# The first of two expert routers: fetching token rows per expert instead of scattering them to slots

## The reference

```python
h = layernorm(x) * (1 + cb) + sb
logits = h @ gate_weight.T                      # 8 experts
probs = softmax(logits)
top1 = argmax(logits)
mask = one_hot(top1, E)
ranks = cumsum(mask, axis=0) - 1                # place of a token in its expert's list
mask = mask * (ranks < C)                       # C = 320 slots per expert, the rest is dropped
dispatch[e, rank] = h[token]                    # 8 x 320 rows
eout = gelu(dispatch @ wi[e]) @ wo[e]           # 256 -> 1024 -> 256
x = x + gb * (probs[top1] * eout[e, rank])      # kept tokens only
```

## Time and profile before

| what | value |
|---|---|
| timed runs, us | 1158.65, 1157.9, 1160.58; median 1158.65 |
| profiled execution, us | 1162.2 |
| its span, first to last instruction, us | 1160.4 |
| TensorE busy | 980.0 us (84%) |
| VectorE busy | 632.0 us (54%) |
| ScalarE busy | 534.2 us (46%) |
| GpSimd busy | 297.8 us (26%) |
| mean granted TensorE clock | 0.929 |

### The profile page before, as it was taken

How to read it: one execution, slowest core, us unless ns; L and a number is a source line. 1 busy time by engine, 2 the same in 40 slices (tenths; PEclk the granted TensorE clock), 3 DMA queues, 4 the chain that set the end, 5 groups by cost and what they waited for, 6 DMA issues and landing times. The chain is left out here.

```text
span 1160.4 us, 24988 instructions
## 1 busy us (share of the span) xinstructions
PE 980.0 (84%) x9918; PEld 635.9 (55%) x9923; DVE 632.0 (54%) x1714; ACT 534.2 (46%) x830; POOL 297.8 (26%) x344
## 2 busy tenths in 40 slices
PE   5889899999999999957099999558657599999994
PEld 3433334445444444433067777346435599999993
DVE  4257999999799797746000000284766533333331
ACT  3523567777866866644023231075055343333330
POOL 3001330011001121320511213245720144545442
PEclk9987999999999999998599999769788799999998
DMA  5753000000002003019315454300055623222223
GB/s 159 174 129 54 2 3 2 3 3 3 2 3 94 3 3 3 3 31 363 99 23 168 108 177 107 84 1 1 0 185 197 209 42 50 45 50 45 50 45 90
DMA packets 71485, 81.65 MB, mean 70 GB/s; under 512 B 21201, under 2 KB 62545, under 8 KB 70689
## 3 DMA queue, kind: packets, MB, share of 16 engines
q1 hardware_dynamic: 58576, 62.75, 19.1%
q0 software_dynamic: 12288, 17.10, 8.4%
q10 hardware_dynamic: 528, 0.52, 0.1%
HBM read 58.19 MB, written 24.13 MB: 71 GB/s over the span
## 5 line engine op out<-in xcount | busy, mean ns | idle before, releaser
L579 ACT ACTIVATE k_prob<-f_s 128x1024 f32<-128x1024 f32 (+3 forms) x320 | 270.1, 896 | 118.5 <-PE f_s L427 117.9
L639 DVE TENSOR_REDUCE k_mpart<-f_r 128x1 f32<-128x512 f32 x384 | 250.6, 685 | 31.7 <-PE f_r L370 29.4
L370 PE MATMUL f_r<-k_ks,k_qs 112*32 112x512 bf16 (+3 forms) x2560 | 212.0, 359 | 16.2 <-DVE k_mpart L639 7.3
L427 PE MATMUL f_s<-k_qs,k_ks 114*32 114x512 bf16 (+3 forms) x2560 | 173.9, 350 | 1.9 <-ACT k_prob L579 1.3
L841 POOL TENSOR_SCALAR_AFFINE_SELECT k_prob<-k_prob 128x256 f32<-128x256 f32 x128 | 51.2, 406 | 400.1 <-ACT k_prob L579 398.9
L443 PE MATMUL f_o<-k_prob,k_vaug 128*32 128x512 f32 (+3 forms) x1280 | 146.5, 531 | 1.5 <-POOL k_prob L841 1.4
L370 PEld LDWEIGHTS f_r<-k_ks,k_qs 112*32 112x32 bf16 x2560 | 69.1, 96 | 135.1 <-DVE k_mpart L639 56.2
L636 DVE CUSTOM_DVE_ANT_0 k_unread<-f_r,k_causal 128x128 bf16<-128x128 f32 (+3 forms) x256 | 121.2, 484 | 21.9 <-PE f_r L370 20.9
L427 PEld LDWEIGHTS f_s<-k_qs,k_ks 114*32 114x32 bf16 x2560 | 64.2, 97 | 79.3 <-issue 27.8
L2002 DVE TENSOR_TENSOR mid<-silu_g,e_u 128x512 f32<-128x512 f32 x39 | 26.8, 688 | 124.7 <-PE e_u L1907 124.7
L1442 DVE SCALAR_TENSOR_TENSOR outr<-p_o,rows,k_mod 128x256 f32<-128x256 f32 x16 | 7.8, 484 | 140.8 <-PE p_o L1399 140.8
(11 more groups left out here) (312 smaller groups left out, 1274.6 us busy)
## 6 DMA issues: line engine op xcount, KB each, us to landing
r_raw<-in_L_ffn_w_dram SPq DMA_DIRECT2D x24, 512.0 KB, 5.8
k_wi<-in_L_ffn_wi_dram SPq DMA_DIRECT2D x8, 1024.0 KB, 5.1
k_wo_e<-in_L_ffn_wo_dram SPq DMA_DIRECT2D x8, 1024.0 KB, 7.5
k_qs<-q_dram SPq DMA_DIRECT2D x6, 768.0 KB, 9.6
sum<-k_x SPq DMA_DIRECT2D x8, 512.0 KB, 9.5
q_dram<-k_room SPq DMA_DIRECT2D x12, 256.0 KB, 4.6
disp<-k_room SPq DMA_DIRECT2D x2, 1310.0 KB, 7.0
rows<-disp SPq DMA_DIRECT2D x8, 262.0 KB, 2.6
```

What stands on the lines that cost most here:

```text
L370: last = nc.tensor.matmul(dst[32 * j:32 * (j + 1), :], qs[0:KROWS, c, GH * g + hs, q0:q0 + 32], ks[0:KROWS, QC * ck:QC * ck + w], start=Tr ...
L427: last = nc.tensor.matmul(sc[h % 2][32 * j:32 * (j + 1), i, off:QC], ks[0:KALL, k0:k0 + 32], qs[0:KALL, c, GH * g + 2 * pair + i, off:QC], ...
L579: nc.scalar.activation(prob[:, u % 2, 2 * pair:2 * pair + 2, off:QC], sc[h % 2][:, :, off:QC], ACT.Exp, scale=HD ** -0.5).then_inc(e_done, 1)
L639: nc.vector.reduce_max(mpart[:, s % 2, hs, t, ck:ck + 1], bank(r)[:, 0:w], AX.X).then_inc(ring_used[r % RING], 1)
```

## The change

The front no longer fills and stores the table `disp`. The function `phase_router` is split. The second layer keeps its part as `phase_router1`, unchanged. The first layer gets `phase_router0`:

- the normalised rows go to `k.h` and from there to `h_rows` in HBM in token order, by four SyncE stores; SyncE's order is now gate weights, expert 0's weights, `wmod`, the four stores, x to the sum, expert 1's weights, the mixing's loads;
- the greatest logit is found by reductions and comparisons over all tiles at once;
- expert and rank give every token a position in a tile of 128 slots (`pos`) and a tile (`blk`, 3 tiles for each of 8 experts); `at_pos` and `at_blk` are the one-hot forms in bf16;
- TensorE sums `at_pos` × codes over all tokens, once for the token number (two codes), once for the weight (three bf16 parts); the last 64 slots of an expert are written to partitions 64 to 127 as well, for the half-width rows of the second product;
- VectorE reads token numbers `tok0`, row numbers `row0` and weights `w0` of all slots;
- GpSimd fetches the rows of experts 0 and 1 from `h_rows` by three indirect loads each, at the end of the router.

In `phase_experts0` SyncE loads weights only, GpSimd issues the three indirect loads of expert e + 2 before the three additions of expert e, and ScalarE begins with a one-column Gelu whose result nobody reads.

```diff
-                for i in range(NT):
-                    nc.gpsimd.indirect_dma_start(
-                        out=k.disp, out_offset=bass.IndirectOffsetOnAxis(ap=scat[:, 0, i:i + 1], axis=0),
-                        in_=hx[:, i, :], in_offset=None).then_inc(sent, 16)
-                pool.wait_ge(sent, 16 * NT)
...
+def gather_rows0(nc, k, e):
+
+    s = e % 2
+    for r, (r0, rn) in enumerate(SLOT_TILES):
+        b = len(SLOT_TILES) * e + r
+        nc.gpsimd.indirect_dma_start(
+            out=k.rows0[0:rn, s, r, :], out_offset=None, in_=k.h_rows,
+            in_offset=bass.IndirectOffsetOnAxis(ap=k.tok0[0:rn, b:b + 1], axis=0)).then_inc(k.rows0_in[s], 16)
...
+            load_weights0(sp, k, a, 0, 0)
+            sp.dma_start(wmod[:, :, :], a.L1_wmod.rearrange("(t p) n -> p t n", p=P)).then_inc(wmod_in, 16)
+            hv = k.h_rows.rearrange("(i p) d -> p i d", p=P)
+            for q in range(NC):
+                sp.wait_ge(h_ready, q + 1)
+                sp.dma_start(hv[:, TQ * q:TQ * (q + 1), :], quarter(k.h, q)).then_inc(kept_h, 16)
...
+            def invert(c0, c1):
+
+                lo = inv_lo[c0][:, 0:NS0 * (c1 - c0)]
+                hi = inv_hi[c0][:, :, :].rearrange("p i e -> p (i e)")[64:128, 0:E * (c1 - c0)].rearrange("p (c e) -> p c e", c=c1 - c0)
+                for i in range(NT):
+                    rhs = code[:, i, c0:c1, :]
+                    nc.tensor.matmul(lo, at_pos[:, i, :], rhs.rearrange("p c b -> p (c b)"),
+                                     start=(i == 0), stop=(i == NT - 1))
+                    last = nc.tensor.matmul(hi, at_pos[:, i, 0:64],
+                                            rhs.rearrange("p c (e r) -> p c e r", r=NST)[:, :, :, NST - 1],
+                                            start=(i == 0), stop=(i == NT - 1), tile_position=(0, 64))
+                return last
...
+            step(nc.vector.tensor_copy(logits[:, :, :], plog[:, :, :]))
+            step(nc.vector.reduce_max(best[:, :], logits[:, :, :], AX.X))
+            step(tt(pri[:, :, :], logits[:, :, :], last_bcast(best[:, :], E), ALU.is_equal))
+            tt(diff[:, :, :], logits[:, :, :], last_bcast(best[:, :], E), ALU.subtract).then_inc(diff_ready, 1)
+            step(tt(pri[:, :, :], pri[:, :, :], bcast(desc[:, :], NT), ALU.mult))
+            step(nc.vector.reduce_max(best[:, :], pri[:, :, :], AX.X))
+            step(tt(one_hot[:, :, :], bcast(desc[:, :], NT), last_bcast(best[:, :], E), ALU.is_equal))
+            nc.vector.tensor_copy(chosen[:, :, :], one_hot[:, :, :]).then_inc(chosen_ready, 1)
...
+            step(tt(at_blk[:, :, :], bcast(iota_b[:, :], NT), last_bcast(blk[:, :], NS0), ALU.is_equal))
+            step(ts(code[:, :, 0, :], at_blk[:, :, :], tok1[:, 0:1], None, ALU.mult))
+            step(tt(code[:, :, 1, :], at_blk[:, :, :], last_bcast(iota_hi[:, :], NS0), ALU.mult))
+            tt(at_pos[:, :, :], bcast(iota_pos[:, :], NT), last_bcast(pos[:, :], P), ALU.is_equal).then_inc(pos_ready, 1)
...
+            for n in range(3):
+                last = tt(code[:, :, 2 + n, :], at_blk[:, :, :], last_bcast(w_part[:, n, :], NS0), ALU.mult)
+            last.then_inc(code_ready, 1)
...
+            dve.wait_ge(tok_done, 1)
+            read(0, 2)
+            step(stt(slot[:, :, :], inv[:, 1, :, :], float(P), inv[:, 0, :, :], ALU.mult, ALU.add))
+            step(ts(row[:, :, :], slot[:, :, :], -1.0, 0.0, ALU.add, ALU.max))
+            nc.vector.tensor_copy(k.tok0[:, :], row[:, :, :].rearrange("p e r -> p (e r)")).then_inc(tok_ready, 1)
...
+            pool.wait_ge(kept_h, 16 * NC)
+            pool.wait_ge(tok_ready, 1)
+            for e in range(2):
+                gather_rows0(nc, k, e)
...
+            nc.scalar.activation(unread[:, :], k.rstd[:, 0:1], ACT.Gelu).then_inc(gelu_done, 1)
...
+            for e in range(E):
+                s = e % 2
+                if e + 2 < E:
+                    pool.wait_ge(t_done, e + 1)
+                    gather_rows0(nc, k, e + 2)
```

More of the change, by code:

```diff
@@ L752, in _ @@
                 rows(s)
[L753 to L765, removed]
         @block.gpsimd
@@ L961, in phase_router @@
         block = ctx.enter_context(nc.Block())
-        KSEL = layer + 1
         @block.sync
@@ L1035, in _ @@
                     pe.wait_ge(hT_ready, 2 * (q - 1))
-                if layer == 1 and q == 2:
-                    pe.wait_ge(w_copied, 6)
-                for last in transpose_quarter(nc, k, rows.h, q, tp[q % 2]):
+                for last in transpose_quarter(nc, k, k.h, q, tp[q % 2]):
                     last.then_inc(tp_done, 1)
@@ L1084, in _ @@
+            pe.wait_ge(lT_ready, NC)
+            pe.wait_ge(pos_ready, 1)
+            invert(0, 2).then_inc(tok_done, 1)
+            pe.wait_ge(code_ready, 1)
+            invert(2, 5).then_inc(weight_done, 1)
         @block.scalar
         def _(act):
[L1086 to L1091 removed]
@@ L1157, in _ @@
-            if layer == 0:
-                chosen_t = one_hot[0]
-            else:
-                chosen_t = chosen
-                step(tt(chosen[:, :, :], one_hot[0][:, :, :], one_hot[1][:, :, :], ALU.add))
-            nc.vector.tensor_copy(chosen_bf[:, :, :], chosen_t[:, :, :]).then_inc(chosen_ready, 1)
-            for j in range(KSEL):
-                step(tt(tmp[j][:, :, :], logits[:, :, :], last_bcast(top[:, :, j], E), ALU.subtract))
-                nc.vector.tensor_scalar_min(tmp[j][:, :, :], tmp[j][:, :, :], 0.0).then_inc(delta_ready, 1)
@@ new lines, in _ @@
+            read(0, 2)
+            step(stt(slot[:, :, :], inv[:, 1, :, :], float(P), inv[:, 0, :, :], ALU.mult, ALU.add))
+            step(ts(row[:, :, :], slot[:, :, :], -1.0, 0.0, ALU.add, ALU.max))
+            nc.vector.tensor_copy(k.tok0[:, :], row[:, :, :].rearrange("p e r -> p (e r)")).then_inc(tok_ready, 1)
+            step(ts(taken[:, :, :], slot[:, :, :], 0.5, None, ALU.is_gt))
+            step(ts(row[:, :, NST - 1], row[:, :, NST - 1], 2.0, upper[:, 0:1], ALU.mult, ALU.add))
+            step(tt(row[:, :, :], row[:, :, :], iota_empty[:, :, :], ALU.subtract))
@@ new lines, in _ @@
+            step(tt(row[:, :, :], row[:, :, :], taken[:, :, :], ALU.mult))
+            step(tt(row[:, :, :], row[:, :, :], iota_empty[:, :, :], ALU.add))
+            step(nc.vector.tensor_copy(k.row0[:, :], row[:, :, :].rearrange("p e r -> p (e r)")))
+            dve.wait_ge(weight_done, 1)
+            read(2, 5)
+            step(tt(inv[:, 2, :, :], inv[:, 2, :, :], inv[:, 3, :, :], ALU.add))
+            step(tt(k.w0[:, :], inv[:, 2, :, :].rearrange("p e r -> p (e r)"),
+                    inv[:, 4, :, :].rearrange("p e r -> p (e r)"), ALU.add))
```

836 lines of the change are left out of this document (455 added, 381 removed).

## The result

The changed kernel took 1153.11 us (median of five runs, 1151.52 to 1153.84) against 1160.58 for the kernel before in runs on the same chip (1157.9 to 1163.96): a ratio of 0.9934, interval 0.9915 to 0.9952. That is faster by 7.5 us, where 13.4 were forecast, and 1153.11 lies outside the range 1143.0 to 1150.5. Part of the distance is the base: the forecast started from 1158.65, the median of three runs, and the kernel before measured 1.9 us more in the five runs here. A range moved up by as much would end at 1152.4, so the measured time would lie outside that too. In a second comparison the same two kernels gave 1153.36 against 1163.43, a ratio of 0.9921 (0.9897 to 0.9945); the two medians alone give 0.9913. The profiled execution took 1153.11 with a span of 1151.2 and a mean clock of 0.932.

The account below looks back on a forecast made before the run. The first router's 34.2 us wait, mostly GpSimd's scatter, was taken as the bound. Chain, inversion, gathers and barrier put the first transpose at 565.3 instead of 578.67, 13.4 us sooner: 1158.65 becomes 1145.3, range 1143.0 to 1150.5.

Parts of the forecast that it names:

- What bounds the kernel: Before the first expert's first transposes, weight loads wait 34.2 us, 20.6 of them GpSimd building scatter descriptors; not TensorE's stretch.
- Up to the position codes: First router: rank product ends at 544.65 as before, then VectorE's work puts the last position code at 552.1.
- The cover: Twelve modulation products ahead of the rank product hide that `chosen` is ready some 2 us sooner; without them 2 us gained.
- The inversion: First router: 32 short TensorE products take at most 2.7 us, hidden behind VectorE's work; token numbers at 556.0.
- The gathers: End of first router: six take 7.3 us, starting 0.5 after VectorE's last number; with 1.0 disturbance GpSimd ends at 564.8.
- the disturbance: VectorE's work beside the first router's gathers lengthens them by 1.0 us, bounds 0 and 1.4.
- The rival of GpSimd held by VectorE: First router's gathers wait until VectorE is done, from 561.5 on; gain only 9.4 us, 1149.3; chance 0.12.
- The barrier: From the gathers' end to the first transpose: 0.5 us, upper bound 1.4; first transpose at 565.3.
- Each later stage starts at a barrier after this one and is not edited: Behind the first router: whatever moves the first transpose at 578.67 moves the rest of the kernel by as much.
- The front: Kernel's start: removing a 2.28 us fill, two stores of zeros and the marks gains zero, at most 2.3 us.
- Gathers spoil the loop: Expert loop: gathers on each expert's path cost 3.8 us seven times, less the 13.4, giving 1171.8; chance 0.03.
- nothing gained: First router: modulation weights land at 552.5 instead of before 539, so the time stays 1158.65; chance 0.02.

Follow-up runs that it names:

- all_late: all_three with VectorE making the weight-code products after the token numbers and its five modulation-row operations in the expert stage: 1140.65 us.
- all_three: Changed kernel with inversion products in two runs, rank products before modulation products, one expert's rows gathered in the router, no GpSimd drain behind the front: 1140.03 us.
- late_mix: all_three with SyncE's eight loads for the mix stage issued at the start of the expert stage instead of the router: 1139.85 us.

## Why the prediction was wrong

**What bounds the kernel: right.** Before the change 34 us at this place were not TensorE's, and removing the scatter gave 9.4 us at the first transpose by two profiles of each kernel (61.99 less 52.54).

**Up to the position codes: right within 0.2 us.** The rank products and the codes came where the sum had them. The cover that the step names, the modulation products, was worth 2.6 us and not 2.

**The inversion: the largest miss, 2.3 us.** The step took 1.34 us for 32 wider products of the second router, doubled it for the lower clock, and called 2.7 an upper bound. Those 32 are all of one shape. The bound holds for one shape (1.21) or for two runs (1.75), and fails for a turn of shapes (4.95). The price of an operation was carried over without its order. Token numbers came at 558.3 in the clock of before, not 556.0.

**The gathers: 7.5 us instead of 8.3 with the disturbance.** Six of them span 7.50 us, and the first started 0.9 behind the numbers, not 0.5. Only the first is longer (1.25, in all profiles but all_late), though VectorE did only operations of 0.2 us beside it. So of the 0.67 us that the step read from the first scatter (1.63) as VectorE's doing, some 0.3 belong to any first transfer of the router; beside the modulation rows (561.87 to 564.81) they took 0.96, 0.95 and 0.91, as later in the expert stage with VectorE idle (0.96, 0.94, 0.91). Half-sized gathers are hardly cheaper, 0.91 against 0.96. The rival of GpSimd held by VectorE is refuted for the modulation rows: no gather was held for the length of a VectorE instruction. In all_late two gathers beside them took 0.08 and 0.19 us more, less than any such instruction (0.43 to 0.75). The rule of the Trainium skill, page "SBUF — State Buffer", section "Who interferes with whom", that one engine blocks fully for the other's whole instruction, was cited beside that rival. The page says so of VectorE's two-port modes alone, so 2.7 us for all five operations was more than it gives; and these rows agree with no full block for any of them.

**The barrier: 2.2 us missed.** The step took 0.42 from the second router, where GpSimd's last indirect transfer was a whole stage back, and its upper bound of 1.4 left the drain out. The experiments put the barrier at 0.54 to 0.72 and the drain behind six gathers at 1.95. Of the second router nothing could be carried over: its drain had been over for 50 us when the block ended.

**"Each later stage starts at a barrier after this one and is not edited": wrong.** The barrier's own price was changed, by eighteen more indirect transfers: a drain of 3.48 us instead of 2.02, so 1.5 us given back at the end of the expert stage. In the loop GpSimd's three more gathers per expert cost nothing, as said; their drain did.

**The front: priced at nothing, worth 2.3 us.** The prediction had it only as an upper bound, since TensorE waits for none of it.

The sum by measured terms: 13.4 − 2.3 (inversion) − 0.4 (start) + 0.8 (gathers) − 2.2 (barrier) = 9.3 at the first transpose; less 1.5 and plus 2.3 makes 10.1. The two comparisons gave 7.5 and 10.1 us by their medians, and by their intervals 5.6 to 9.9 and 6.4 to 12. The terms fit the second and lie just above the upper end of the first; what made the first lower stays open. That the forecast of 13.4 came within a factor of two of either is partly luck: 2.3 us that it had put at nothing made up for one of the terms that it missed.

**Rivals.** "Gathers spoil the loop" and "nothing gained" did not happen. Rows landed in time, SyncE had issued its last load before the gathers ended, and the early Gelu table delayed no copy.

## What to carry to other kernels

Ask of a cost taken from another stage in which order its instructions stood: short products that take turns between weight loads of 128 and of 64 columns cost nearly three times what the same products cost in two runs. Count indirect transfers also against the end of their block: here each adds 0.082 us to a drain. It costs time where the barrier waits for it, is free where another engine comes later, and if skipped is paid at the next block that drains. Where semaphores already guard the data, barriers without it took 4.6 us off the kernel before (by the interval 3.5 to 6.6) and, from one comparison to another, 4.5 us off the changed one (1153.36 to 1148.9). When the time between two stages grows and nothing in it was edited, look at what the barrier waits for: the drain's own record is in the trace.

## What the runs showed of the hardware

- 32 bf16 products, 16 with 128 and 16 with 64 weight columns, all over 128 rows, at clock 0.50: 4.95 us in turn, 1.75 in two runs, 1.21 when all have 128 columns. With the clock at 1.00 two runs took 1.17 us (all_three).
- GpSimd's drain at the end of a block: 0.06 us and 0.082 for each indirect transfer since the last drain, over 16 (1.36 us), 24, 42, 45, 48 and 78 of them (6.41), also when they have landed; right behind six or three gathers it ends 2.0 to 2.1 us after the last.
- An indirect gather of 64 rows of 1 KB lands 1.97 us after GpSimd has issued it, DMA share 0.35 (late_mix).
